# Eight edits to a transformer kernel: weights laid out ahead of the launch, and four changes of order

## The reference, cut to what matters

```python
x = x + attn_a(layernorm(x), w_qkv, w_out, rel_bias)     # 16 heads of 64, relative bias
x = x + ffn(layernorm(x), Wr, br, ln_g, ln_b, W1, b1, W2, b2)
x = x + attn_b(layernorm(x), w_kv_down, w_kv_up, w_q, w_out)  # causal, 16 heads of 64, one latent for k and v
x = x + ffn(layernorm(x), ...)                            # the same weights again

# attn_a
qkv = x @ w_qkv.T; q, k, v = qkv.reshape(b, t, dh, 3, h).transpose(3, 0, 4, 1, 2)
attn = softmax(q @ k.T * scale + bias);  out = (attn @ v) @ w_out.T

# ffn: each token goes to the one expert of eight with the largest router probability
idx = argmax(softmax(xt @ Wr + br)); gate = max(...)
y = gate * (relu(norm(xt) @ W1[idx] + b1[idx]) @ W2[idx] + b2[idx])
```

## Time and profile before

| | us |
|---|---|
| three runs | 649.43, 650.32, 650.25 |
| median | 650.25 |
| the profiled execution | 648.84 |
| its span, first to last instruction | 647.6 |

### The profile page before, as it was taken

The page is one execution under the profiler, slowest core; times in us unless marked ns, Lnnn a source line. Parts: engine busy times, 40 slices in busy tenths (PEclk is TensorE's granted clock), DMA queues, the critical chain, the costliest instruction groups (busy, mean ns, idle before and its releaser), DMA issues.

```text
span 647.6 us, 22119 instructions
## 1 busy us (share of the span) xinstructions
PE 625.2 (97%) x7454; PEld 537.3 (83%) x7454; DVE 511.1 (79%) x2211; ACT 524.6 (81%) x1776; POOL 354.9 (55%) x674
## 2 busy tenths in 40 slices
PE   5999999999999999999999899999999999999997
PEld 4678787877878788879988789888888988888997
DVE  4986878778887888888865787887988799898833
ACT  3898888889788878785675998998989898986664
POOL 5653645455475557643206554555757665772746
PEclk9999999999999999999999999999999999999999
DMA  8999989999991000133531100000000000113140
GB/s 263 317 307 308 289 211 319 313 310 311 282 287 41 3 2 27 43 100 83 166 107 37 40 3 3 8 2 6 7 7 21 16 4 2 36 49 93 55 129 18
DMA packets 90319, 74.78 MB, mean 115 GB/s; under 512 B 12225, under 2 KB 87111, under 8 KB 90080
## 3 DMA queue, kind: packets, MB, share of 16 engines
q1 hardware_dynamic: 86512, 66.24, 36.6%
q0 software_dynamic: 2848, 6.33, 3.0%
q10 hardware_dynamic: 848, 0.79, 0.4%
HBM read 19.93 MB, written 54.00 MB: 114 GB/s over the span
## 4 chain that ended last, share of the span: by engine, by line
PE 79%; DVE 7%; issue 4%; POOL 3%; ACT 3%; DMA 3%; SPq 1%; DVEq 0%; POOLq 0%; ACTq 0%
PE ps L578 16%; PE ps L694 13%; PE ps L742 13%; PE ps L573 10%; PE ps L575 8%; PE ps L574 8%; PE ps L848 5%; PE ps L864 4%; DVE ring L1365 2%; ACT ring L1046 2%; DMA T<-in_bias 1%; POOL out L449 1%; POOL ring L429 1%; PE ps L780 1%; DVE v L1330 1%
## 5 line engine op out<-in xcount | busy, mean ns | idle before, releaser
L429 POOL TENSOR_SCALAR ring<-ring,rs 128x256 f32<-128x256 f32 (+1 forms) x500 | 217.1, 451 | 129.4 <-DVE rs L1378 127.5
L1046 ACT ACTIVATE ring<-ring,mn 128x256 f32<-128x256 f32 (+1 forms) x512 | 243.7, 483 | 1.5 <-DVE mn L1365 1.4
L578 PE MATMUL ps<-ident,ring 128*128 128x128 f32 x896 | 122.0, 275 | 3.6 <-DVE ol L1337 1.8
L578 PEld LDWEIGHTS ps<-ident,ring 128*128 128x128 f32 x896 | 101.9, 142 | 12.5 <-issue 4.1
L694 PE MATMUL ps<-qk 64*64 64x256 f32 (+3 forms) x2048 | 107.1, 344 | 1.3 <-ACT qk L1018 0.8
L742 PE MATMUL ps<-pt,v 64*64 64x256 f32 (+3 forms) x2048 | 102.9, 338 | 2.0 <-ACT pt L1034 1.5
L1046 ACT ACTIVATION_READ_ACCUMULATOR ring<-ring,mn 128x1 f32 x512 | 101.7, 199 | 0.0
L742 PEld LDWEIGHTS ps<-pt,v 64*64 64x64 f32 x2048 | 76.5, 133 | 26.1 <-ACT pt L1034 6.6
L1393 DVE COPY pt<-ps 128x512 f32<-128x512 f32 (+1 forms) x128 | 75.5, 589 | 20.3 <-PE ps L578 18.8
L694 PEld LDWEIGHTS ps<-qk 64*64 64x64 f32 x2048 | 65.0, 133 | 28.4 <-issue 12.3
L1018 ACT COPY qk<-ps 128x512 f32<-128x512 f32 x128 | 74.3, 580 | 12.4 <-PE ps L575 12.2
(11 more groups left out here) (210 smaller groups left out, 1297.3 us busy)
## 6 DMA issues: line engine op xcount, KB each, us to landing
xs_scratch<-f_ys SPq DMA_DIRECT2D x16, 2064.0 KB, 21.5
yr_scratch<-f_ys SPq DMA_DIRECT2D x8, 1024.0 KB
f_xs<-xs_scratch SPq DMA_DIRECT2D x50, 129.0 KB, 2.3
w<-in_W SPq DMA_DIRECT2D x16, 256.0 KB, 6.0
xs_scratch<-f_ys SPq DMA_DIRECT2D x2, 1677.0 KB, 20.5
yr_scratch<-f_ys SPq DMA_DIRECT2D x25, 64.0 KB, 1.8
T<-in_bias SPq DMA_DIRECT2D x2, 512.0 KB, 8.2
T<-in_bias SPq DMA_DIRECT2D x1, 1024.0 KB, 10.7
```

Of the source, the lines that this page charges most:

```text
L429: i = pool.tensor_scalar(part, part, rs[:, q], 1.0, ALU.mult, ALU.mult)
L578: return pe.transpose(out, src, ident if order is None else order)
L1046: i = act.activation(part, part, ACT.Exp, bias=mn[:, q], scale=-1.0, accum_out=sm[:, q])
```

## The change

It has eight parts.

- The weights `w_qkv`, `w_out_a`, `w_q`, `w_kv_up`, `w_out_b` are laid out by numpy before the launch. They are loaded as they are used, by one DMA each, or for `w_qkv` by five: three panels of query and key weights (`PANELS`, for units 0 to 1, 2 to 3 and 4 to 7) and two halves of value weights. The PE transposes of weights go, ACT and DVE read the weights from SBUF.
- ACT issues panels 0 and 2 and the two value halves, SP panel 1, ahead of the bias table.
- The bias table's last MB comes in two DMAs, with `w_out` between them.
- ACT splits panels 0 and 1 ahead of the input of batch 0, panel 2 behind it. DVE splits panel 0 ahead of `xh`, panel 1 behind it, and panel 2 in step 2, with the second value half.
- In the last routing, `place` stands ahead of the copy of table 9, and its sum `run` behind the row numbers.
- On SP the gathers of tiles 12 to 19 stand ahead of the reading of row numbers 20 to 24, in both stages.
- On ACT the second batch's input stands ahead of a copy of values in the second stage.
- The first `keep` on ACT waits for `w_out`'s low part, since `won` shares its memory with `oh`.

```diff
+PANELS = [(0, 2), (2, 4), (4, 8)]
 # tables_at
-    for k in (n - 1, n) if n == N_LATE + 1 else () if n == N_LATE else (n,):
+    for k in {N_LATE: (), N_LATE + 1: (n - 1,), N_LATE + 2: (n - 1, n)}.get(n, (n,)):
 # PE begin and step: the transposes of weights go
-            for n in range(4):
-                if n % 2 == 0:
-                    pe.wait_ge(d_wqk[n // 2], 64)
-                pe_weights(n)
-            if st == 0 and s == 0:
-                value_weights()
-            if st == 0:
-                extra(s)
 # ACT
         def begin():
+            products(0, 1, 2, 3)
             pre_b(0)
-            products(0, 1, 2)
+            products(4, 5)
-            if st == 0 and s == 1:
-                value_weights()
+            if st == 0 and s in (1, 2):
+                value_weights(s - 1)
...
+            if st and pre_at(s, "b", st) == 1:
+                pre_b(1)
             for v in VALUES[st].get(s, ()):
                 values(*v)
-            if (b := pre_at(s, "b", st)) is not None:
+            if (b := pre_at(s, "b", st)) is not None and (b != 1 or not st):
                 pre_b(b)
 # ACT's DMAs
-        for g in range(2):
-            for j, w in enumerate((wqn, wkn)):
-                act.dma_start(w[64:128, 4 * g:4 * g + 4, :], heads(j, 1, 2 * g, 2 * g + 2)).then_inc(d_wqk[g], 16)
-        act.dma_start(wvn[64:128, :, :], heads(2, 1, 0, 4)).then_inc(d_wv, 16)
+        for g in (0, 2):
+            act.dma_start(raw(g), t["w_qkv"][:, panel(g)]).then_inc(d_wqk[g], 16)
+        for g in range(2):
+            act.dma_start(wvn[g][:, 0:512], t["w_qkv"][:, 2048 + 512 * g:2560 + 512 * g]).then_inc(d_wv[g], 16)
 # DVE, place
-            dve.tensor_tensor(run[:, :], c[:, 1, n - 1, :], bas[:, n - 1, :], ALU.add).then_inc(v_c, 1)
-            v_n[0] += 1
+            if t1 < NT:
+                dve.tensor_tensor(run[:, :], c[:, 1, n - 1, :], bas[:, n - 1, :], ALU.add).then_inc(v_c, 1)
+                v_n[0] += 1
...
             dve.tensor_copy(posi[:, t0:t1], posf[:, 0:n]).then_inc(v_pos, 1)
+            if t1 == NT:
+                dve.tensor_tensor(run[:, :], c[:, 1, n - 1, :], bas[:, n - 1, :], ALU.add).then_inc(v_used, 1)
 # DVE begin and step
             pre_a(0)
+            products(0, 1)
             pre_a2(0)
+            products(2, 3)
             pre_b(0)
-            products(0, 1, 2)
-            if st == 0 and s == 1:
-                value_weights()
+            if st == 0 and s in (1, 2):
+                value_weights(s - 1)
+            if st == 0 and s == 2:
+                products(4, 5)
 # SP
-        for g in range(2):
-            for j, w in enumerate((wqn, wkn)):
-                sp.dma_start(w[0:64, 4 * g:4 * g + 4, :], heads(j, 0, 2 * g, 2 * g + 2)).then_inc(d_wqk[g], 16)
-        sp.dma_start(wvn[0:64, :, :], heads(2, 0, 0, 4)).then_inc(d_wv, 16)
+        sp.dma_start(raw(1), t["w_qkv"][:, panel(1)]).then_inc(d_wqk[1], 16)
         sp.dma_start(a_T[:, 0:4, :], t["bias"][:, 0:4, :]).then_inc(d_T[0], 16)
...
-        sp.dma_start(won[:, :], t["w_out_a"]).then_inc(d_won, 16)
-        sp.dma_start(a_T[:, 8:16, :], t["bias"][:, 8:16, :]).then_inc(d_T[2], 16)
+        sp.dma_start(a_T[:, 8:12, :], t["bias"][:, 8:12, :]).then_inc(d_T[2], 16)
+        sp.dma_start(won[:, :, :], t["w_out_a"]).then_inc(d_won, 16)
+        sp.dma_start(a_T[:, 12:16, :], t["bias"][:, 12:16, :]).then_inc(d_T[3], 16)
...
+        sp.dma_start(bq[:, :], t["w_q"]).then_inc(d_bq, 16)
+        sp.dma_start(bu[:, :], t["w_kv_up"]).then_inc(d_bu, 16)
...
         rows(0, 2, 3, 4, 5)
+        gather(0, 1, 3, 4, 5)
         rows(0, 3, 6, 7)
-        gather(0, 1, 3, 4, 5)
```

More of the change, by code:

```diff
@@ L263, in build @@
     pre = ExitStack()
[L264 removed]
+    raws = at_first(pre, *(sb(n, [128, 1024], scope=pre) for n in ("wqkn0", "wvn0", "wqkn1", "wvn1")))
+    wqkn, wvn = raws[0::2], raws[1::2]
     a_ring = [sb(f"ring{i}", [128, 2, 4, 2, 64], scope=base) for i in range(4)]
@@ L293, in build @@
     base.close()
-    d_wqk, d_wv, d_x, d_won = [sem("d_wqk0"), sem("d_wqk1")], sem("d_wv"), [sem(f"d_x{i}") for i in range(3)], sem("d_won")
-    d_T, d_wr, d_ln = [sem(f"d_T{i}") for i in range(3)], sem("d_wr"), sem("d_ln")
+    d_wqk, d_wv = [sem(f"d_wqk{g}") for g in range(len(PANELS))], [sem("d_wv0"), sem("d_wv1")]
+    d_x, d_won = [sem(f"d_x{i}") for i in range(3)], sem("d_won")
+    d_T, d_wr, d_ln = [sem(f"d_T{i}") for i in range(4)], sem("d_wr"), sem("d_ln")
     d_empty, d_clear = [sem(f"d_empty{st}") for st in range(2)], sem("d_clear")
@@ L328, in build, with panel, raw @@
     xv = t["x"].rearrange("b (s p) d -> p (b s) d", p=128)
[L329 to L337, removed]
+    def panel(g):
+        a, b = PANELS[g]
+        return slice(256 * a, 256 * b)
+    def raw(g):
+        a, b = PANELS[g]
+        return wqkn[a // 4][:, 256 * (a % 4):256 * (a % 4) + 256 * (b - a)]
     def load(engine, values, a, b, most):
@@ L658, in QK @@
                 key_ready(b)
-            if st == 0 and u in (0, 4):
-                pe.wait_ge(a_m, 2 + u // 2)
-                pe.wait_ge(v_m, 2 + u // 2)
+            for g, (first, _) in enumerate(PANELS):
+                if st == 0 and u == first:
+                    pe.wait_ge(a_m, 2 * g + 2)
+                    pe.wait_ge(v_m, 2 * g + 2)
             if U0 + u:
@@ L974, in w_part, with w_raw, halves @@
         g, j = divmod(n, 2)
-        return w[:, 1024 * j + 512 * g:1024 * j + 512 * g + 512]
+        a, b = PANELS[g]
+        return w[:, 1024 * j + 128 * a:1024 * j + 128 * b]
+    def w_raw(n):
+        g, j = divmod(n, 2)
+        a, b = PANELS[g]
+        c = 256 * (a % 4) + 128 * j * (b - a)
+        return wqkn[a // 4][:, c:c + 128 * (b - a)]
+    def halves(w, g):
+        return w[:, 512 * g:512 * g + 512]
     def w_scale(n):
@@ L1352, in S @@
                 dve.wait_ge(p_set, k_T0)
+            if st == 0 and u in (1, 3):
+                dve.wait_ge(v_wv, (u + 1) // 2)
+            if st == 0 and u == 2:
+                dve.wait_ge(v_m, 2 * len(PANELS))
             if st == 0 and u in (2, 4, 6):
@@ L1571, in begin, with value_weights @@
             pre_a(0)
+            products(0, 1)
             pre_a2(0)
+            products(2, 3)
             pre_b(0)
-            products(0, 1, 2)
-        def value_weights():
-            for g in range(2):
-                low(by_parity(wvl[:, :])[:, 4 * g:4 * g + 4], by_unit(ps[4 + g][:, :]),
-                    by_parity(wvh[:, :])[:, 4 * g:4 * g + 4], a_wv, g + 1, v_wv)
+        def value_weights(g):
+            low(halves(wvl, g), wvn[g][:, 0:512], halves(wvh, g), a_wv, g + 1, v_wv)
         def step(s):
@@ L1811, in sp_program @@
         rows(1, 2, 3, 4, 5)
+        gather(1, 1, 3, 4, 5)
         rows(1, 3, 6, 7)
-        gather(1, 1, 3, 4, 5, 6, 7)
+        gather(1, 1, 6, 7)
         for i in range(NY):
@@ L1831, with _by_units, _by_halves, _w_qkv @@
           "L0_ffn_ln_b": "ln_b", "L0_ffn_W1": "W1", "L0_ffn_b1": "b1", "L0_ffn_W2": "W2", "L0_ffn_b2": "b2"}
+def _by_units(a):
+    return a.reshape(128, 4, 2, 2, 64).transpose(0, 1, 3, 2, 4).reshape(128, 1024)
+def _by_halves(a):
+    return a.reshape(128, 4, 2, 2, 64).transpose(0, 2, 1, 3, 4).reshape(128, 1024)
+def _w_qkv(a):
+    q, k, v = a.reshape(64, 3, 1024 // 64, 128).transpose(1, 3, 2, 0).reshape(3, 128, 1024)
+    q, k = _by_units(q), _by_units(k)
+    panels = [w[:, 128 * a:128 * b] for a, b in PANELS for w in (q, k)]
+    return np.concatenate(panels + [_by_halves(v)], axis=1)
+_LAYOUT = {"w_qkv": _w_qkv,
+           "w_out_a": lambda a: a.reshape(128, 8, 128).transpose(2, 1, 0),
+           "w_q": _by_units,
+           "w_kv_up": lambda a: np.concatenate([_by_units(a[:, :1024]), _by_halves(a[:, 1024:])], axis=1),
+           "w_out_b": lambda a: a.reshape(8, 128, 128).transpose(1, 0, 2)}
 def kernel(**inputs):
@@ L1845 @@
     for name in _INS:
-        a = np.ascontiguousarray(inputs[name])
-        give(_SHORT[name], a)
+        a = inputs[name]
+        give(_SHORT[name], np.ascontiguousarray(_LAYOUT[_SHORT[name]](a) if _SHORT[name] in _LAYOUT else a))
     rel = np.ascontiguousarray(inputs["L0_attn_a_rel_bias"])
```

93 lines of the change are left out of this document (30 added, 63 removed).

## The result

| | before | after |
|---|---|---|
| runs | 4 | 4 |
| median, us | 650.23 | 655.35 |
| lowest to highest | 649.43 to 650.32 | 653.92 to 656.11 |
| the profiled execution | 648.84 | 654.76 |
| its span | 647.6 | 653.4 |

The change made the kernel slower: ratio 1.0084, 95% interval 1.0062 to 1.0105, some 5 us. I forecast 1.5 us faster.

What follows compares the result with a forecast made beforehand. Bound by waits for weights and table, then DVE up to `pt` at 27.67, then PE. Gains 1.1 (start, 2.2 minus 1.1 given back) + 0.3 + 0.1 = 1.5 us off 650.25: 648.75, range 647.4 to 650.7.

Steps and rivals of the forecast that it cites:

- the first scores: Start, unit 0 on DVE: first scores begin at 13.25 instead of 15.44, a gain of 2.2 us.
- Reading SBUF in place of PSUM I cost at nothing: DVE's weight splits at the start: a piece of 512 takes 0.6 to 0.7 us either way, so zero cost.
- The eight transposes of `w_out` that vanish at that place give nothing: PE ahead of 28.32: PE has slack there, so removing transposes costing about 0.9 us gains zero.
- PE reaching the `pt` wait later than DVE: Sign of a wrong forecast, at DVE's copy `pt`: PE's lost transposes would count after all.
- The slow pace at the start: Rival, chance 0.22: PE's slow pace lasts through the first scores, 16 matmuls need 1.96 instead of 0.98; total 650.25.
- `xh` near 6.2: Start, DVE: `xh` begins at 6.25 instead of 5.23, 1.0 us later, behind its two low parts of panel 0.
- First query matmul: Start, PE: with weights already in SBUF it begins at 8.6 instead of 10.84, 2.2 us earlier.
- Given back behind the scores, 1.1: DVE behind 15.44: a value half and two panel 2 pieces, 0.6 each, replace one of 0.69; 1.1 us lost.
- Panel 2 and the table: Start, DMAs: panel 2 lands at 8.5 with no wait; table lands at 7.6 to 11.2, its work mostly hidden.
- The slower rival of panel 2: Rival, chance 0.08: panel 2's split delays ACT's first `qk`, each us past 9.05 lost; beyond 11.85, 651.6 or more.
- Step 4 of the second stage, 0.3: Second batch's input ahead of a values copy on ACT: `xth` 0.58 earlier, PE gains 0.3, bounds 0 and 0.59.
- Between the layers, 0.1: Last routing, gathers, reading of row numbers and fewer weight DMAs: 0.1 us gained together.

Runs made afterwards that it cites:

- before_wout_sbuf: Kernel before with `w_out` alone laid out by numpy and split from SBUF, without its eight PE transposes: 654.42 us beside 649.64, ratio 1.0074.
- late_only: Kernel before with only the changes behind the first attention's start; that start stays as it was: 649.23 us beside 649.88, ratio 0.9988.
- best_wvh_early: `lows_first_busy_pe` with ACT's first value half moved ahead of its first `qk`: 646.67 us beside 650.02 for the kernel before, ratio 0.9948.
- lows_first_busy_pe: Changed kernel, POOL's last subtraction a step later, DVE's panel 2 and second value-half low parts before first scores, identity transposes on PE at start: 646.83 us, 0.9956.
- best_again: `lows_first_busy_pe` unaltered, run once more: 646.70 us beside 650.22 for the kernel before, ratio 0.9950.
- after_busy_pe: Changed kernel plus identity transposes into an unused bank where PE waits, 24 of them ahead of `xh`'s: 652.58 us beside 649.88 for the kernel before, ratio 1.0049.
- best_x_alone: `lows_first_busy_pe` with ACT's panel 2 and value-half DMAs and SP's behind `x` held until `x`'s first batch landed: 651.05 us beside 650.02, ratio 1.0009.

## Why the prediction was wrong

At 34 us I expected a gain of 1.1 and the trace shows a loss of 5.6. The difference of 6.7 is the sum of three terms: 2.3 that the first scores did not gain, 3.0 of DVE waiting for POOL, and 1.5 of slow clock behind `pt` (0.45 at four transposes, 1.0 at the scores).

- **"Reading SBUF in place of PSUM I cost at nothing"** is the step that failed. The pieces compared had taken 0.6 to 0.7 either way, but where POOL's subtraction ran they read PSUM. From SBUF the same pieces cost 2.0 and 2.4 beside it: 1.3 at the value half and 1.7 at `wo`, 3.0 on the path. The rows for it were in the trace of before, where `wo`'s low parts and POOL's piece overlapped free of charge (below). The Trainium skill ("SBUF — State Buffer", "Who interferes with whom") says that a DVE instruction with two SBUF inputs contends with a GpSimd instruction that reads SBUF, and that the one issued second blocks; the traces agree, with the numbers above. I had not weighed it. Where DVE read one operand from PSUM, it took 1.29 beside POOL's 1.89. That agrees with the same section of the Trainium skill, by which a DVE instruction with at most one SBUF input, outside the modes that use both ports, doesn't contend.

```profile
26.38 1.29 DVE L1232 TENSOR_TENSOR wo<-ps,wo 128x512 fp32r<-128x512 f32 x2
26.53 1.89 POOL L459 TENSOR_TENSOR T<-cT,T 128x1024 f32<-128x1024 f32 x1
```

- **"The eight transposes of `w_out` that vanish at that place give nothing"**: this step failed too. PE had slack there, and I took slack for free. The pause before `pt`, with the transposes gone and DVE late, is followed by 1.2 GHz. In the changed kernel that cost 1.5 in the trace, in `before_wout_sbuf` 1.7 in the trace and some 3 by the medians, and no term of the sum held it. How much of it the missing transposes alone would cost was not tested. I had weighed the clock for the start alone. The sign that I gave for this case, PE reaching the `pt` wait later than DVE, did not show: PE waited 2.22 there, and the loss came through the pause.
- **The slow pace at the start** was the rival at 0.22, and it came true: 16 matmuls took 2.1 and not 1.05. It was priced at 650.25 because I took its gain elsewhere as safe.
- **`xh` near 6.2**: 6.91. DVE's low parts of panel 0 did not hold it. `x` landed at 4.99 and not 3.35, for which I had no term. ACT's wait of 1.57 for panel 1 was off the path, since ACT then stood 0.61 for PE ahead of `xth`. First query matmul 9.55 against 8.6: 0.7 from `xh`, 0.3 from the hand-over of `xtl` to PE. ACT's table load began at 2.71 and not at 3.7, which bought nothing. These 1.0, 0.3 in the second unit's queries (1.58 for six matmuls against 1.25) and 1.05 of slow scores make the 2.3 between 13.25 and 15.53.
- **Given back behind the scores, 1.1**: the pieces were 0.6 each, as said, plus POOL's 1.3.
- **Panel 2 and the table**: landed in time (split at 8.63, table used at 9.64, no wait), as said. The slower rival of panel 2 had the right sign and the wrong mechanism.
- **Step 4 of the second stage, 0.3**: 0.27 in both traces. Right.
- **Between the layers, 0.1**: `late_only` puts all late edits at 0.65, against 0.4, within its interval. The gathers' landing moves by half a us either way between executions, so single figures there tell little: the changed kernel lost 0.34 at 320, where `late_only` won 0.49.

## What to carry to other kernels

Before a split or a subtraction on DVE is given a second SBUF operand, look what POOL reads from SBUF in the same stretch, even if DVE's operation costs the same alone; here moving POOL's piece by one step took 2.8 us off the changed kernel. Before work is taken from PE because "it has slack", read the pause that is left and what follows it: here a pause of 2.2 to 2.9 us, from the missing transposes and the late DVE together, cost 1.5 to 1.7 us of slow clock in the traces and more by the medians. Where an edit speeds up one chain, ask which engine is dense right behind it; here the gain was that of ACT's third `qk`, not that of DVE's first scores.

## What the runs showed of the hardware

- DVE and POOL took strict turns: with POOL's piece running, DVE's ended half a us behind it (2.38 for 0.69), and POOL's took 0.4 more when DVE had begun first (2.30 for 1.89). DVE operations with one operand in PSUM paid nothing (1.29 for two beside POOL's 1.89 in the kernel before). It holds for small operations too: POOL's `full_e` of 128x96, 0.26 long in the kernel before, took 1.34 in the changed kernel, where it began with DVE's 1.22 us subtraction of the bias table.
- The clock column says 1.00 at the start when PE is slow. For the changed kernel it reads 1.00 in every stretch from 8 to 16, though 256-column matmuls stood 0.21 apart at 9.9 to 13.1; the first change of clock is recorded at 15.13. In `best_wvh_early` the same pace, slow from 9 to 12.5, reads 0.50 in 10 to 12, since a change stood ahead of it. Ahead of the first change the spacing of like matmuls is the reading to trust.
- The clock can fall again after added work. With 24 transposes from 1.65 on, the first change was recorded at 5.4 to 6.8 in five traces. The clock stayed up through the first scores in three of them (`lows_first_busy_pe`, `best_again`, `after_busy_pe`). It fell at 9.07 in `best_wvh_early`, behind pauses of PE of 0.84 and 0.81, where `lows_first_busy_pe` had 0.61 and 0.81 and kept it, and at 9.49 in `best_x_alone`, behind a pause of 2.19.
- With the same instructions PE becomes fast at different moments. In the five traces with the old start and no work added ahead of it the first change lies at 10.49, 12.72, 13.31, 13.47 and 15.22, and DVE's first scores between 14.96 and 16.57. In the five with laid-out weights and no work added it lies between 15.13 and 17.85, and the first scores between 15.20 and 15.53. So one pair of traces tells the gain at the first scores only to about a us: by the medians the laid-out weights brought them 0.4 earlier, where the pair above says 0.1 later.
